# A twelve-stage network on one core: moving a four-bit feed-forward beside the attention that follows it

## The chip, the cores and the metric

The kernel runs on one core of a Trainium2 chip. The metric is the device time of one execution in microseconds. Three runs of the kernel before have a median of 1778.88 us (1777.74 to 1781.62).

## The reference

The network adds twelve sublayers, one after the other, to a residual stream `x` of 2048 tokens by 128 features, in float32. The change lies in two of them, the four-bit feed-forward of the third layer and the linear attention that opens the fourth. Cut to what matters:

```python
def fp4_linear(x, w):
    xq = fp4_quant_dequant(x)      # blocks of 16, scale = max|x| / 6, round to {0, .5, 1, 1.5, 2, 3, 4, 6}
    wq = fp4_quant_dequant(w)
    return jnp.einsum('bsk,nk->bsn', xq, wq)
gate = fp4_linear(x, w_gate)       # 128 -> 352
y = fp4_linear(x, w_up)            # 128 -> 352
h = jax.nn.silu(gate) * y
return fp4_linear(h, w_down)       # 352 -> 128

# the attention behind it
q, k, v = x @ Wq + bq, x @ Wk + bk, x @ Wv + bv          # 128 -> 8 heads of 64
attn = softmax(sum(q_t * k_t) * scale, over heads)       # one weight for each head and token
new_state = decay * state + (1 - decay) * attn * v_t
out = (q * states + sigmoid(q * aug_param)) @ Wo + bo    # then a layer norm
```

Then follow a sublayer that multiplies `sigmoid(r)`, with `r` the normalised stream, by rows that were computed earlier (receptance), and a sparse expert stage with 14 experts.

## The kernel before

All of it is one function, `l2_ffn_and_l3`. The 16 blocks of 128 tokens are taken in four quads of 512 tokens (`NQ = 4`, `QUAD = 4`), and each engine has a program of its own, written out by hand: TensorE makes products and transposes, VectorE (`dve`) rounds, scans and takes statistics, the scalar engine (`act`) copies from PSUM and evaluates sigmoid, silu, exp and gelu, and POOL does the elementwise work left over. An engine works through its program in order. It waits for the others at semaphores: `after(engine, semaphore, n)` and `wait_ge`. So the order of the work is the order of the calls in these four programs.

For a quad `f` the feed-forward goes: `round_x` (eight steps on VectorE: scale, inverse, scaled, step twice, add, subtract), `scale_x_up` (POOL), `turn_x` (four transposes), `take_x` (copy), then for each of the four blocks `gate_up` (line 2698: a gate and an up product, 352 wide), `silu` and `times_gate` (VectorE, line 3052). Gate has bank 5 and up bank 6. Then the rounding of the hidden quad, 1408 wide (`hidden_scales`, `find_steps`, `round_off`, lines 3024 to 3035), `scale_hidden_up` (POOL), `down` (transposes and the 352-row product, line 2718) and `add_down` (line 3061), which adds to `x` and computes the variance for the attention's norm (`spreads`, `variances`, line 239).

The attention of a quad `q`: `turn_attended`, `queries_keys` (lines 2746 and 2747: four chunks of 128 features, two products of 512 columns each), `multiply` (VectorE, line 3109: a key chunk plus bias times the query chunk), scores (line 2755), copy to `s_row`, a small transpose, `subtract_top`, exponential, `shares`, transpose, copy to `probsT`; then for each of the four chunks a value product (2762), a product that spreads the probabilities over the features (2782), and `scan` (VectorE, lines 3128 to 3133: product, recurrence, times query). `add_aug` (POOL) adds the sigmoid; `project` (lines 2727 and 2729) is the output product of one block, four products and a bias row; `take_out`, `stats`, `out_scale`, `apply` and `add_out` (three 128x512 operations on POOL) are its norm. `shifts`, `receptance` and `receive` are the receptance sublayer, and `received_normals` prepares the expert stage.

The feed-forward runs one quad ahead of the attention. At the head of quad `q` the products of the feed-forward for quad `q + 1` and the output product of quad `q - 1` alternate:

```python
for q in range(NQ):
    if q < LAST:
        turn_x(q + 1)
    for j in range(QUAD):
        if q < LAST:
            gate_up(q + 1, j)
        if q > 0:
            project(q - 1, j)
    turn_attended(q)
    queries_keys(q)
    attend(q)
```

`attend(q)` holds `down(q + 1)` between its second and third chunk. After the last quad come `turn_tokens(0)`, `rate(0)` and `first(0, 0)` of the expert stage, the output product of quad 3, and the experts, `second(q, e)` and `first(q, e + 2)` in turn.

## Time and profile before

| what | value |
|---|---|
| median of 3 runs | 1778.88 us |
| the profiled execution | 1774.92 us |
| its span | 1773.1 us |
| TensorE busy (matmuls) | 1524.3 us, 86% |
| TensorE busy with weight loads | 978.7 us, 55% |
| VectorE busy | 1166.1 us, 66% |
| scalar engine busy | 900.9 us, 51% |
| POOL busy | 717.1 us, 40% |

The span is that of the instructions; the execution's own time is 1.8 us longer. Busy shares are averages over twelve sublayers. The function of this case starts at 1272 us of the span; its loop over quads with the lead-in reaches to 1553 us, and the expert stage fills the rest. The hidden quad lies in the tile `w_l_xattn`, the rounded input and the gate values in `ctx`, which are free by then. Matmuls of float32 are shown with two instructions for each product. PE in a view is TensorE, DVE is VectorE, ACT is the scalar engine. A clock of 1.00 is the full 2.4 GHz and 0.50 is 1.2 GHz. In a timeline the bracket at the end says how long the engine had been idle and which instruction released it.

### The profile page before, as it was taken

The numbers are of one execution on the slowest core, as the hardware profiler recorded it, in microseconds if no ns is written. First come the engines' busy times: TensorE is split into PE (matmuls) and PEld (weight loads), VectorE is DVE, ScalarE is ACT, GpSimd is POOL, SyncE is SP. The second block draws the span as 40 slices with busy tenths as digits, with TensorE's granted clock in tenths as the row PEclk, the third lists the DMA queues.
The fourth block names the chain that finished last, engine by engine and source line by source line (L and its number), as shares of the span: only waits on it lengthen the run. The fifth ranks groups of instructions, "written<-read, shape, count | busy, mean of one in ns | idle before, by whom it ended". The sixth has DMA issues, their size and how long they took to land. (4 is left out here: it accounts for less than half of the span.)

```text
span 1773.1 us, 28878 instructions
## 1 busy us (share of the span) xinstructions
PE 1524.3 (86%) x10011; PEld 978.7 (55%) x10011; DVE 1166.1 (66%) x2471; ACT 900.9 (51%) x2612; POOL 717.1 (40%) x674
## 2 busy tenths in 40 slices
PE   4998858789799998979999879999758876789998
PEld 2565535445577765533333358888533443367776
DVE  4887572479687865548989877777636557544443
ACT  2774432267577752247777647776513322444442
POOL 2566341122664433138888953333401235412000
PEclk8999987989999999979999999999857877899999
DMA  6000000000000000020000000000000000000000
GB/s 279 2 2 1 1 1 1 0 1 2 1 2 1 2 1 1 1 85 1 1 1 1 1 1 2 1 2 2 1 1 0 1 1 1 1 1 7 7 1 13
DMA packets 3166, 18.96 MB, mean 11 GB/s; under 512 B 593, under 2 KB 721, under 8 KB 2257
## 3 DMA queue, kind: packets, MB, share of 16 engines
q1 hardware_dynamic: 3024, 17.14, 2.4%
q8 instruction: 81, 1.33, 0.3%
q14 instruction: 61, 0.49, 0.1%
HBM read 16.09 MB, written 1.05 MB: 10 GB/s over the span
## 5 line engine op out<-in xcount | busy, mean ns | idle before, releaser
L827 POOL TENSOR_TENSOR l_xattn_probs<-l_xattn_probs,l_xattn_recip 128x512 f32<-128x512 f32 x128 | 133.0, 1039 | 223.2 <-DVE l_xattn_recip L766 222.8
L999 ACT ACTIVATE l_attn_probs<-ps,l_attn_neg_max 128x128 f32<-128x128 f32 x512 | 144.7, 383 | 74.4 <-DVE l_attn_neg_max L1048 74.1
L2547 POOL TENSOR_TENSOR l_mamba_hc<-l_mamba_h,l_mamba_c 128x512 f32<-128x512 f32 x128 | 159.0, 1269 | 0.0
L2449 DVE TENSOR_TENSOR_SCAN l_mamba_h<-ps,l_mamba_dBx 128x512 f32<-128x512 f32 x128 | 152.7, 1213 | 1.8 <-ACT ps L2346 0.7
L2219 PE MATMUL ps<-l_mamba_hc,w_const 128*128 128x512 f32 x256 | 136.5, 637 | 19.5 <-POOL l_mamba_hc L2547 16.5
L3160 DVE SCALAR_TENSOR_TENSOR xn<-ps,l_gates,xn 128x128 f32<-128x128 f32 x224 | 63.1, 345 | 119.1 <-PE ps L2831 118.2
L761 DVE COPY l_xattn_probsT<-ps 128x512 f32<-128x512 f32 x128 | 88.0, 687 | 71.5 <-PE ps L613 71.5
L2960 ACT ACTIVATE wkv<-ps,w_early 128x512 f32<-128x512 f32 x112 | 70.7, 683 | 115.5 <-PE ps L2820 115.5
L2831 PEld LDWEIGHTS ps<-w_early,wkv 128*128 128x128 f32 x896 | 109.1, 194 | 26.1 <-issue 18.7
L2831 PE MATMUL ps<-w_early,wkv 128*128 128x128 f32 x896 | 111.4, 278 | 6.2 <-ACT wkv L2960 6.2
L712 ACT ACTIVATE l_xattn_probs<-ps,l_xattn_neg_max 128x128 f32<-128x128 f32 x256 | 91.7, 389 | 41.5 <-DVE l_xattn_neg_max L756 41.5
L2820 PE MATMUL ps<-xnT,w_early 128*128 128x512 f32 x224 | 107.8, 605 | 0.0
L712 ACT ACTIVATE l_xattn_probs<-l_xattn_biased,l_xattn_neg_max 128x128 f32<-128x128 f32 x256 | 99.3, 391 | 12.2 <-DVE l_xattn_neg_max L756 12.2
L2346 ACT ACTIVATE ps<-l_mamba_th,l_mamba_a_bias,l_mamba_a_scale 128x508 f32<-128x508 f32 x128 | 97.1, 781 | 14.1 <-DVE l_mamba_h L2449 13.8
L1048 DVE TENSOR_REDUCE l_attn_neg_max<-ps 128x8 f32<-128x1024 f32 x64 | 78.0, 1221 | 32.6 <-PE ps L904 32.6
L245 POOL TENSOR_TENSOR rs<-rs,neg_half 128x4 f32<-128x4 f32 (+2 forms) x28 | 39.4, 1407 | 143.3 <-DVE rs L239 143.3
L2219 PEld LDWEIGHTS ps<-l_mamba_hc,w_const 128*128 128x128 f32 x256 | 44.4, 193 | 86.9 <-POOL l_mamba_hc L2547 70.0
L613 PE MATMUL ps<-w_const,l_xattn_probs 128*128 128x128 f32 x512 | 82.2, 284 | 9.6 <-DVE l_xattn_probsT L761 5.1
L613 PEld LDWEIGHTS ps<-w_const,l_xattn_probs 128*128 128x128 f32 x512 | 57.7, 143 | 51.4 <-issue 39.3
L904 PE MATMUL ps<-l_attn_k_one,l_attn_q 32*128 32x512 f32 x256 | 77.3, 699 | 8.1 <-POOL l_attn_k_one L1079 4.5
L2540 POOL TENSOR_TENSOR l_mamba_dBx<-l_mamba_dtx,l_mamba_b 128x512 f32<-128x512 f32 x48 | 60.9, 1270 | 56.6 <-DVE l_mamba_dtx L2409 36.1
L915 PEld LDWEIGHTS ps<-w_const,l_attn_probs 128*128 128x128 f32 x512 | 58.3, 146 | 42.7 <-issue 28.3
(524 smaller groups left out, 3690.2 us busy)
## 6 DMA issues: line engine op xcount, KB each, us to landing
w_early<-in_l_moe SPq DMA_DIRECT2D x1, 3669.0 KB, 11.5
w_l_xattn<-in_l_xattn SPq DMA_DIRECT2D x1, 2176.0 KB, 22.5
w_early<-in_l_xattn SPq DMA_DIRECT2D x1, 1890.0 KB, 15.1
w_l_attn<-in_l_attn SPq DMA_DIRECT2D x1, 1242.0 KB, 24.5
ctx<-in_ctx SPq DMA_DIRECT2D x1, 1088.0 KB, 10.8
x<-in_x SPq DMA_DIRECT2D x2, 512.0 KB, 4.4
ctxT<-in_ctxT SPq DMA_DIRECT2D x1, 1024.0 KB, 8.9
out_x<-x SPq DMA_DIRECT2D x4, 256.0 KB, 2.2
```

The costliest lines, as they stand in the source:

```text
L613: mm = nc.tensor.transpose(T_of(n)[:, g * P:(g + 1) * P], probs[:, D % 2, n, g, :], G.c["ident"])
L712: ins = nc.scalar.activation(probs[:, D % 2, n, g, :], values, ACT.Exp, bias=neg_max[:, D % 2, n, g:g + 1], accum_out=row_sum[:, D % 2, n, ...
L761: nc.vector.tensor_copy(probsT[:, D % 2, n, :, :], heads4(T_of(n))).then_inc(copied, 1)
L827: nc.gpsimd.tensor_tensor(probs[:, D % 2, n, :, :], probs[:, D % 2, n, :, :], along(recip[:, D % 2, n, :], [P, HALF, P]), ALU.mult).then_i ...
L999: ins = nc.scalar.activation(probs[:, t % 4, g, :], S_of(t)[:, g * P:(g + 1) * P], ACT.Exp, bias=neg_max[:, t % 2, g:g + 1], accum_out=total)
L1048: nc.vector.tensor_reduce(neg_max[:, t % 2, :], by_head(S_of(t), 8), AX.X, ALU.max, negate=True).then_inc(maxed, 1)
L2219: nc.tensor.matmul(G.ps[:, SUM_BANK[half], :], G.c["ident"], hc[:, t % 4, half, :], start=False, stop=n == NS - 1).then_inc((sum0, sum1)[h ...
L2346: nc.scalar.activation(bank4(DA_BANK[half])[:, :, 1:], th[:, q % 2, half, :, 1:], ACT.Exp, scale=a_scale[:, half, n:n + 1], bias=a_bias[:, ...
L2449: nc.vector.tensor_tensor_scan(flat(h[:, t % 2, half, :, :]), G.ps[:, DA_BANK[half], :], flat(dBx[:, t % 2, half, :, :]), 0.0, ALU.mult, A ...
L2547: nc.gpsimd.tensor_tensor(heads4(hc[:, t % 4, half, :]), h[:, t % 2, half, :, :], c_sb[:, t % 3, :, :], ALU.mult).then_inc((hc0_set, hc1_s ...
L2820: mm = nc.tensor.matmul(G.ps[:, 2 * (e % 2) + c, :], we["w1"][:, (e * EC + c) * P:(e * EC + c + 1) * P], G.xnT[:, quad(q), :], start=True, ...
L2831: mm = nc.tensor.matmul(G.ps[:, Y_BANK[e % 2], j * P:(j + 1) * P], hidden[:, e % 2, c, j * P:(j + 1) * P], we["w2"][:, (e * EC + c) * D:(e ...
```

## The change

The arithmetic is the same. What moves:

- Gate and up products get two pairs of banks, (5, 6) and (4, 7). Block 1 may start without block 0 having been taken; block `j > 1` waits for `times_gate` of block `j - 2` and so on (`h_made`). `turn_x` writes bank 4 instead of 7.
- Quad 1's gate products are made before the loop. In the loop `turn_x(q + 2)` and the gate products of quad `q + 2` stand in `attend(q)`, behind the third and fourth spread of the probabilities. The feed-forward's gate products are thus two quads ahead.
- `project(q - 1, ...)` stands between the chunks of `queries_keys(q)`. Its bias is one product, 512 columns wide, ahead of the blocks.
- On VectorE the rounding steps of the hidden quad stand between the four `multiply` steps; `round_x` comes before the first scan, `stats` behind the rounding, `apply` between `subtract_top` and `shares`, and `times_gate` around the last scan.
- On the scalar engine the four sigmoids (`aug`, now with four buffers) come ahead of `s_row`; `receptance(q - 2)` stands behind `s_row`. The receptance of quad 2 comes in the expert stage, right before that of quad 3.
- On POOL `scale_hidden_up` is first in a quad, `receive(q - 2)` stands ahead of `add_out(q - 1)`, and `attended_normals` behind the second `add_aug`.
- `scale_down` and `round_off` are cut into `find_scales`, `scale_down`, `add_steps` and `take_steps_off`, with the same instructions; `x_step` is the head of `h_step`.

```diff
@@ -2689,17 +2690,22 @@
     def turn_x(f):
         pe.wait_ge(x_rounded, f + 1)
-        after(pe, f_added, f)
+        after(pe, p_copied, f - 1)
+        after(pe, h_made, QUAD * f)
         for j in range(QUAD):
             mm = nc.tensor.transpose(G.ps[:, X_BANK, j * P:(j + 1) * P], xq[:, j * P:(j + 1) * P], G.c["ident"])
         mm.then_inc(x_turned, 1)
     def gate_up(f, j):
         pe.wait_ge(x_copied, f + 1)
-        after(pe, h_made, QUAD * f + j)
-        after(pe, h_copied, QUAD * f)
-        nc.tensor.matmul(G.ps[:, G_BANK, 0:I], xqT[:, j * P:(j + 1) * P], wgT, start=True, stop=True)
-        nc.tensor.matmul(G.ps[:, U_BANK, 0:I], xqT[:, j * P:(j + 1) * P], wuT, start=True, stop=True).then_inc(gu_made, 1)
+        if j == 0:
+            after(pe, h_copied, QUAD * f)
+        if j == 1:
+            after(pe, f_added, f)
+        if j > 1:
+            pe.wait_ge(h_made, QUAD * f + j - 1)
+        nc.tensor.matmul(G.ps[:, G_BANK[j % 2], 0:I], xqT[:, j * P:(j + 1) * P], wgT, start=True, stop=True)
+        nc.tensor.matmul(G.ps[:, U_BANK[j % 2], 0:I], xqT[:, j * P:(j + 1) * P], wuT, start=True, stop=True).then_inc(gu_made, 1)
     def turn_hidden(f, j):
         pe.wait_ge(h_rounded, f + 1)
...
@@ -2722,11 +2728,14 @@
     def project(q, j):
         pe.wait_ge(o_set, CH * (q + 1))
-        pe.wait_ge(p_copied, q + 1)
+        if j == 0:
+            pe.wait_ge(p_copied, q + 1)
+            pe.wait_ge(h_made, QUAD * min(q + 3, NQ))
+            nc.tensor.matmul(G.ps[:, O_BANK, :], G.c["ones_row"], w["bo"].unsqueeze(1).broadcast_to([1, QUAD, D]), start=True,
+                             stop=False, skip_group_check=True)
         for c in range(CH):
-            nc.tensor.matmul(G.ps[:, O_BANK, j * P:(j + 1) * P], o[:, c, j * P:(j + 1) * P],
-                             w["wo"][:, c * D:(c + 1) * D], start=c == 0, stop=False)
-        mm = nc.tensor.matmul(G.ps[:, O_BANK, j * P:(j + 1) * P], G.c["ones_row"], w["bo"], start=False, stop=True)
+            mm = nc.tensor.matmul(G.ps[:, O_BANK, j * P:(j + 1) * P], o[:, c, j * P:(j + 1) * P],
+                                  w["wo"][:, c * D:(c + 1) * D], start=False, stop=c == CH - 1, skip_group_check=True)
         if j == QUAD - 1:
             mm.then_inc(out_made, 1)
...
+            if c > 0 and q > 0:
+                project(q - 1, c - 1)
             after(pe, qk_set, CH * q + max(c - 1, 0))
             nc.tensor.matmul(G.ps[:, Q_BANK[c % 2], :], w["wq"][:, c * P:(c + 1) * P], G.xnT[:, quad(q), :], start=True, stop=True)
             nc.tensor.matmul(G.ps[:, K_BANK[c % 2], :], w["wk"][:, c * P:(c + 1) * P], G.xnT[:, quad(q), :], start=True, stop=True)\
               .then_inc(q_made, 1)
+        if q > 0:
+            project(q - 1, QUAD - 1)
     def attend(q):
-        after(pe, out_copied, q)
-        for c in range(CH):
-            pe.wait_ge(qk_set, CH * q + c + 1)
-            mm = nc.tensor.matmul(G.ps[0:H, S_BANK, :], w["heads"][:, c * H:(c + 1) * H], qk[:, c, :], start=c == 0,
-                                  stop=c == CH - 1)
-        mm.then_inc(s_made, 1)
         def v(c):
             after(pe, fed_set, CH * q + max(c - 1, 0))
...
               .then_inc(v_made, 1)
         v(0)
+        after(pe, out_copied, q)
+        pe.wait_ge(h_made, QUAD * min(q + 2, NQ))
+        for c in range(CH):
+            pe.wait_ge(qk_set, CH * q + c + 1)
+            mm = nc.tensor.matmul(G.ps[0:H, S_BANK, :], w["heads"][:, c * H:(c + 1) * H], qk[:, c, :], start=c == 0,
+                                  stop=c == CH - 1)
+        mm.then_inc(s_made, 1)
+        v(1)
         pe.wait_ge(s_copied, q + 1)
         for j in range(QUAD):
             mm = nc.tensor.matmul(G.ps[:, T_BANK, j * H:(j + 1) * H], s_row[:, j * P:(j + 1) * P],
                                   G.c["ident"][0:H, 0:H], start=True, stop=True)
         mm.then_inc(s_turned, 1)
-        v(1)
         pe.wait_ge(p_set, q + 1)
         for j in range(QUAD):
             mm = nc.tensor.transpose(G.ps[0:H, T_BANK, j * P:(j + 1) * P], probs[:, j, :], G.c["ident"])
@@ -2777,10 +2791,17 @@
         for c in range(CH):
             if c == 2 and q < LAST:
                 down(q + 1)
+            if c == 2 and q + 2 < NQ:
+                turn_x(q + 2)
             if c >= 2:
                 v(c)
             nc.tensor.matmul(G.ps[:, P_BANK[c % 2], :], sel_e[:, c * P:(c + 1) * P], probsT[:],
                              start=True, stop=True).then_inc(p_made, 1)
+            if c >= 2 and q + 2 < NQ:
+                gate_up(q + 2, c - 2)
+        if q + 2 < NQ:
+            gate_up(q + 2, 2)
+            gate_up(q + 2, 3)
     def turn_tokens(q):
         pe.wait_ge(m_normed, QUAD * (q + 1))
...
     down(0)
+    turn_x(1)
+    for j in range(QUAD):
+        gate_up(1, j)
     for q in range(NQ):
-        if q < LAST:
-            turn_x(q + 1)
-        for j in range(QUAD):
-            if q < LAST:
-                gate_up(q + 1, j)
-            if q > 0:
-                project(q - 1, j)
         turn_attended(q)
         queries_keys(q)
...
@@ -2921,8 +2938,14 @@
         ins.then_inc(r_set, 1)
     def attend(q):
+        act.wait_ge(q_set, CH * (q + 1))
+        after(act, o_set, CH * q)
+        for c in range(CH):
+            nc.scalar.activation(aug[:, c, :], q_sb[:, c, :], ACT.Sigmoid, scale=w["aug"][:, c:c + 1]).then_inc(aug_set, 1)
         act.wait_ge(s_made, q + 1)
         nc.scalar.copy(s_row[:], G.ps[0:H, S_BANK, :]).then_inc(s_copied, 1)
+        if q > 1:
+            receptance(q - 2)
         act.wait_ge(shifted, q + 1)
         nc.scalar.activation(probs[:], probs[:], ACT.Exp, scale=DH ** -0.5).then_inc(exped, 1)
         act.wait_ge(p_turned, q + 1)
@@ -2930,15 +2953,17 @@
         for c in range(CH):
             if c == 2 and q < LAST:
                 take_hidden(q + 1)
+            if c == 2 and q + 2 < NQ:
+                take_x(q + 2)
             act.wait_ge(v_made, CH * q + c + 1)
             after(act, fed_set, CH * q + max(c - 1, 0))
             nc.scalar.activation(v_sb[:, c % 2, :], G.ps[:, V_BANK[c % 2], :], ACT.Identity,
                                  bias=fresh_bv[:, c:c + 1], scale=fresh[:, c:c + 1]).then_inc(v_set, 1)
-            after(act, o_set, CH * q + max(c - 1, 0))
-            nc.scalar.activation(aug[:, c % 2, :], q_sb[:, c, :], ACT.Sigmoid, scale=w["aug"][:, c:c + 1])\
-              .then_inc(aug_set, 1)
-        if q > 0:
-            receptance(q - 1)
...
             if e == 5:
                 take_gates(q)
             if (q, e) == (0, 5):
+                receptance(LAST - 1)
                 receptance(LAST)
             if e == 10 and q < LAST:
                 take_tokens(q + 1)
...
-    round_off(h_scaled, h_step, h_evened)
+    add_steps(h_scaled, h_step)
+    take_steps_off(h_scaled, h_step, h_evened)
     scale_up(blocks(old[:, 0:QUAD * I]), h_scaled, h_scale[:], h_evened, 0, h_rounded)
     add_down(0)
+    times_gate(1, 0)
     normals(0)
+    for j in range(1, QUAD):
+        times_gate(1, j)
     for q in range(NQ):
         f = q + 1
         if f < NQ:
-            for j in range(QUAD):
-                times_gate(f, j)
+            hidden_scales(f)
+        multiply(q, 0)
+        if f < NQ:
+            hidden_down()
+        multiply(q, 1)
+        if f < NQ:
+            find_steps(h_scaled, h_step)
+        multiply(q, 2)
+        if f < NQ:
+            add_steps(h_scaled, h_step)
+        multiply(q, 3)
+        if f < NQ:
+            take_steps_off(h_scaled, h_step, h_evened)
         if q > 0:
             stats(q - 1)
-        multiply(q)
+        subtract_top(q)
         if q > 0:
             apply(q - 1)
-        if f < NQ:
-            hidden_scales(f)
-        subtract_top(q)
-        if f < NQ:
-            find_steps(h_scaled, h_step)
         shares(q)
-        if f < NQ:
-            round_off(h_scaled, h_step, h_evened)
+        if f + 1 < NQ:
+            round_x(f + 1)
+        scan(q, 0)
+        scan(q, 1)
         if q > 1:
             received_spreads(q - 2)
-        scan(q, 0)
-        scan(q, 1)
-        if f + 1 < NQ:
-            round_x(f + 1)
+        if f < NQ:
+            add_down(f)
+        scan(q, 2)
         if q > 0:
             attended_spreads(q - 1)
-        scan(q, 2)
-        if f < NQ:
-            add_down(f)
+        if f + 1 < NQ:
+            times_gate(f + 1, 0)
         scan(q, 3)
         if f < NQ:
             normals(f)
+        if f + 1 < NQ:
+            for j in range(1, QUAD):
+                times_gate(f + 1, j)
     below_max(0)
     for q in range(NQ):
         best_two(q)
...
@@ -3310,30 +3359,32 @@
     attended_normals(0)
     for q in range(NQ):
         f = q + 1
+        if f < NQ:
+            scale_hidden_up(f)
         if q > 0:
             out_scale(q - 1)
+        if q > 1:
+            receive(q - 2)
+        if q > 0:
             add_out(q - 1)
+        if f + 1 < NQ:
+            scale_x_up(f + 1)
+        add_aug(q, 0)
+        add_aug(q, 1)
         if f < NQ:
-            scale_hidden_up(f)
+            attended_normals(f)
+        add_aug(q, 2)
+        if q > 0:
+            shifts(q - 1)
+        add_aug(q, 3)
         if q > 1:
             received_normals(q - 2)
-        add_aug(q, 0)
-        add_aug(q, 1)
-        if f + 1 < NQ:
-            scale_x_up(f + 1)
-        if q > 0:
-            shifts(q - 1)
-        add_aug(q, 2)
-        add_aug(q, 3)
-        if f < NQ:
-            attended_normals(f)
-        if q > 0:
-            receive(q - 1)
     out_scale(LAST)
     add_out(LAST)
     shifts(LAST)
+    receive(LAST - 1)
+    receive(LAST)
     received_normals(LAST - 1)
-    receive(LAST)
     received_normals(LAST)
```

TensorE before, at the end of quad 0's attention (value product 2762, spread 2782) and the head of quad 1 (`turn_x` 2694, gate and up 2701 and 2702, output product 2727 and 2729):

```order
L2762 MATMUL ps<-xnT,w_l_attn 128x512
L2782 MATMUL ps<-l_probsT,w_const 128x512
L2694 MATMUL ps<-w_const,ctx 128x128 x4
L2701 MATMUL ps<-w_l_mamba,l_xqT 128x352
L2702 MATMUL ps<-w_l_mamba,l_xqT 128x352
L2727 MATMUL ps<-w_l_attn,l_o 128x128 x4
L2729 MATMUL ps<-w_l_attn,ones 128x128
L2701 MATMUL ps<-w_l_mamba,l_xqT 128x352
L2702 MATMUL ps<-w_l_mamba,l_xqT 128x352
L2727 MATMUL ps<-w_l_attn,l_o 128x128 x4
```

The same place now (`turn_x` 2696, value 2767, spread 2798, gate and up 2707 and 2708):

```order
L2696 MATMUL ps<-w_const,ctx 128x128 x4
L2767 MATMUL ps<-xnT,w_l_attn 128x512
L2798 MATMUL ps<-l_probsT,w_const 128x512
L2707 MATMUL ps<-w_l_mamba,l_xqT 128x352
L2708 MATMUL ps<-w_l_mamba,l_xqT 128x352
L2767 MATMUL ps<-xnT,w_l_attn 128x512
L2798 MATMUL ps<-l_probsT,w_const 128x512
L2707 MATMUL ps<-w_l_mamba,l_xqT 128x352
L2708 MATMUL ps<-w_l_mamba,l_xqT 128x352
L2707 MATMUL ps<-w_l_mamba,l_xqT 128x352
L2708 MATMUL ps<-w_l_mamba,l_xqT 128x352
```

The gate and up products lie ahead of the transpose of the attended quad in both, but the output product has gone from between them. It now stands behind that transpose (2747), with its bias (2734) ahead of the first block (2737), between the query and key products (2757, 2758):

```order
L2747 MATMUL ps<-w_const,xn 128x128 x4
L2757 MATMUL ps<-xnT,w_l_attn 128x512
L2758 MATMUL ps<-xnT,w_l_attn 128x512
L2734 MATMUL ps<-w_l_attn,ones 128x512
L2737 MATMUL ps<-w_l_attn,l_o 128x128 x4
L2757 MATMUL ps<-xnT,w_l_attn 128x512
L2758 MATMUL ps<-xnT,w_l_attn 128x512
L2737 MATMUL ps<-w_l_attn,l_o 128x128 x4
L2757 MATMUL ps<-xnT,w_l_attn 128x512
```

VectorE before, at the head of quad 1, from the four key products on (`multiply` 3109, `apply` 3089, scales 3024 to 3027, `subtract_top` 3115):

```order
L3109 SCALAR_TENSOR_TENSOR l_qk<-ps,w_l_attn,l_q 128x512 x4
L3089 TENSOR_SCALAR l_out<-l_out,l_small 128x128 x4
L3024 TENSOR_REDUCE l_h_scale<-w_l_xattn 128x88
L3025 TENSOR_SCALAR l_h_scale<-l_h_scale 128x88
L3026 RECIPROCAL l_h_inverse<-l_h_scale 128x88
L3027 SCALAR_TENSOR_TENSOR w_l_xattn<-w_l_xattn,l_h_inverse 128x1408
L3115 TENSOR_REDUCE l_top<-ps 128x4
```

and now (scales 3048 and 3049, `multiply` 3144, `scale_down` 3054 and 3055, steps 3058 to 3065):

```order
L3048 TENSOR_REDUCE l_h_scale<-w_l_xattn 128x88
L3049 TENSOR_SCALAR l_h_scale<-l_h_scale 128x88
L3144 SCALAR_TENSOR_TENSOR l_qk<-ps,w_l_attn,l_q 128x512
L3054 RECIPROCAL l_h_inverse<-l_h_scale 128x88
L3055 SCALAR_TENSOR_TENSOR w_l_xattn<-w_l_xattn,l_h_inverse 128x1408
L3144 SCALAR_TENSOR_TENSOR l_qk<-ps,w_l_attn,l_q 128x512
L3058 TENSOR_SCALAR w_l_xattn<-w_l_xattn 128x1408
L3059 TENSOR_SCALAR w_l_xattn<-w_l_xattn 128x1408
L3144 SCALAR_TENSOR_TENSOR l_qk<-ps,w_l_attn,l_q 128x512
L3062 TENSOR_TENSOR w_l_xattn<-w_l_xattn 128x1408
L3144 SCALAR_TENSOR_TENSOR l_qk<-ps,w_l_attn,l_q 128x512
L3065 TENSOR_TENSOR w_l_xattn<-w_l_xattn 128x1408
```

The key products are spread over the rounding, and the rounding's last step comes before the maximum of the scores instead of after the shares.

## Rows read from the trace of the kernel before

**Rows 1.** Stages: busy (instructions) of PE, PEld, DVE, ACT, POOL, then clock.

```profile
1319.66:1374.26 54.60, 43.27 (x113) 20.75 (x112) 32.60 (x54) 17.81 (x32) 10.11 (x8) 0.72 0.00 1
1374.26:1432.96 58.70, 42.78 (x153) 23.29 (x151) 40.25 (x83) 20.25 (x38) 18.57 (x16) 0.82 0.00 0
1432.96:1492.64 59.68, 45.18 (x148) 25.01 (x148) 39.19 (x85) 20.08 (x36) 25.70 (x22) 0.79 0.00 1
1492.64:1553.48 60.84, 46.89 (x153) 27.32 (x153) 25.76 (x66) 17.87 (x27) 26.97 (x24) 0.74 0.00 1
```

**Rows 2.** Timeline of VectorE, lead-in: start, duration, line, tiles [idle before].

```profile
1290.00 0.52 DVE L3052 TENSOR_TENSOR w_l_xattn<-ctx,ps 128x352 f32<-128x352 f32 x1 [3.36 <-ACT ctx L2889]
...
1298.33 1.62 DVE L3024 TENSOR_REDUCE l_h_scale<-w_l_xattn 128x88 f32<-128x1408 f32 x1
...
1307.80 1.62 DVE L3040 TENSOR_TENSOR w_l_xattn<-w_l_xattn,l_h_scale 128x1408 f32<-128x1408 f32 x1
```

**Rows 3.** Groups by line of VectorE in round 1, 1374.26 to 1432.96.

```profile
L3109 DVE SCALAR_TENSOR_TENSOR l_qk<-ps,w_l_attn,l_q 128x512 f32<-128x512 f32 x4 | 3.0, 751 | 4.5 <-ACT l_q L2907 4.5
...
L3052 DVE TENSOR_TENSOR w_l_xattn<-ctx,ps 128x352 f32<-128x352 f32 x4 | 2.1, 518 | 8.6 <-ACT ctx L2889 8.6
```

**Rows 4.** Timeline of TensorE in rounds 1 and 2.

```profile
1387.96 0.86 PE L2701 MATMUL ps<-w_l_mamba,l_xqT 128*128 128x352 f32 x2
...
1389.24 1.05 PE L2727 MATMUL ps<-w_l_attn,l_o 128*128 128x128 f32 x8
...
1394.65 1.02 PE L2747 MATMUL ps<-xnT,w_l_attn 128*128 128x512 f32 x2
...
1399.23 3.60 PE L2755 MATMUL ps<-l_qk,w_l_attn 128*8 128x512 f32 x8
...
1444.73 1.54 PE L2701 MATMUL ps<-w_l_mamba,l_xqT 128*128 128x352 f32 x2
...
1447.24 1.92 PE L2727 MATMUL ps<-w_l_attn,l_o 128*128 128x128 f32 x8
```

**Rows 5.** Timeline of VectorE, end of round 1.

```profile
1420.92 0.68 DVE L3024 TENSOR_REDUCE l_x_scale<-xn 128x32 f32<-128x512 f32 x1
...
1425.80 0.87 DVE L3094 BATCH_NORM_STATS2 st<-x 128x6 f32<-128x128 f32 x4
...
1427.76 0.69 DVE L3128 TENSOR_TENSOR l_fed<-l_v,ps 128x512 f32<-128x512 f32 x1
...
1430.35 0.68 DVE L3061 TENSOR_TENSOR x<-x,ps 128x512 f32<-128x512 f32 x1
```

**Rows 6.** Timeline of the scalar engine.

```profile
1412.55 1.28 ACT L2938 ACT_TABLE_LOAD   x1
1413.85 0.72 ACT L2938 ACTIVATE l_aug<-l_q,w_l_attn 128x512 f32<-128x512 f32 x1
...
1430.56 1.65 ACT L2920 ACTIVATE l_r<-x,l_shift,rs 128x128 f32<-128x128 f32 x4 [5.48 <-POOL l_shift L3290]
```

**Rows 7.** Timeline of TensorE, last output product and sixth expert.

```profile
1547.04 1.59 PE L2727 MATMUL ps<-w_l_attn,l_o 128*128 128x128 f32 x8
...
1584.18 3.78 PE L2831 MATMUL ps<-w_early,wkv 128*128 128x128 f32 x16 [6.17 <-ACT wkv L2960]
```

**Rows 8.** Timelines of POOL and VectorE: operations beside each other and alone.

```profile
1356.38 2.59 POOL L3257 TENSOR_TENSOR w_l_xattn<-w_l_xattn,l_h_scale 128x1408 f32<-128x1408 f32 x1 [33.86 <-DVE w_l_xattn L3035]
...
1439.59 1.26 POOL L3294 TENSOR_TENSOR l_r<-l_r,ctxT 128x512 f32<-128x512 f32 x1
...
1357.36 2.69 DVE L3131 TENSOR_TENSOR_SCAN l_state<-l_keep,l_fed 128x512 f32<-128x512 f32 x1
...
1428.48 1.22 DVE L3131 TENSOR_TENSOR_SCAN l_state<-l_keep,l_fed 128x512 f32<-128x512 f32 x1
```

**Rows 9.** TensorE timeline before its gate products, then its clock over 4 us.

```profile
1431.18 1.09 PE L2694 MATMUL ps<-w_const,ctx 128*128 128x128 f32 x4 [6.66 <-DVE x L3061]
...
1444.00:1448.00 4.00, 4.00 (x11) 0.50 0.02 4
```

58 lines of the change are left out of this document (35 added, 23 removed).

## Prediction

> **What bounds the kernel now.** I read the busy time of the engines by stage, then TensorE's and VectorE's order of time through one quad, then the clock. The page's chain names lines but not rounds, so I cut the span myself: a round runs from the end of one quad's variance (line 239, the last step of `spreads` behind `add_down`) to the next quad's. In the rounds of 54.6, 58.7 and 59.7 us no engine is full [rows 1]: VectorE is busy 40.25 of 58.7 us, TensorE 42.8, and a good part of that at half clock. The rounds are bound by a chain that crosses the engines one at a time. [rows 2] shows one link: VectorE sits 3.4 us before a gate product (L3052), because one pair of banks holds gate and up, so the next pair of products waits for it. In round 1 VectorE loses 8.6 us before those four products and 4.5 us before the key products (L3109), waiting for the scalar engine, which waits for TensorE [rows 3]; that is most of its idle 18 us.
>
> TensorE's costs come at two rates [rows 4]. A gate/up pair goes from 1444.73 to 1447.24, 2.5 us, at half clock, and 1.3 us at full (1387.96 to 1389.24). A token block of the output product is 1.05 us at full clock, about twice that at half; its bias row goes on top. A query/key pair takes 1.7 us at full clock (two products of 1.02 that overlap by 0.16), some 3.5 at half. The scores take 3.6 us. The serial piece on VectorE has its marks in [rows 5]: x rounding 1420.92 to 1425.80 (4.9 us), the spreads of another quad 1425.80 to 1427.76 (1.9), a scan step 1427.76 to 1430.35 (2.6), `add_down` with its variance from 1430.35 to the round's end at 1432.96 (2.6). The rounding of a hidden quad, scales included, took 1298.33 to 1307.80, 9.5 [rows 2].
>
> **The change, part by part.** All times from the profiled execution, 1774.92 us.
>
> Lead-in. With two pairs of banks, quad 0's gate products no longer alternate with VectorE. Today the last ends just before the reduction at 1298.33 [rows 2]. Now four pairs run back to back, held only by VectorE, which is free at 1286.1: product 0 ends 1286.6, pair 2 1289.1, pair 3 1291.6 (2.5 us each at half clock), then 0.6 for the sigmoid and 0.5 for the product: 1292.7. **-5.6 us**.
>
> Round 0 (54.6 now). Quad 1's pairs start at 1318.1 behind quad 0's output, before the variance, and end at +8.4 of the round rather than +13.6. Then the attended transpose and copy (1.3), and the first query/key pair at full clock (+11.3; TensorE has been busy without a gap since +0). The rounding steps now stand between key products: VectorE's queue there holds 3.0 of key products and 9.5 of rounding; the last key product is at +20.8, its score at +21.8. Before `s_row` the scalar engine must now load a table and do four sigmoids, 1.28 + 4 x 0.7 (they overlap to 4.1) [rows 6]: it is free at +22.5. So scores leave at +23.1, 1.5 later the maximum is off, then exponential, shares (+25.6), x rounding 4.9, two scans 5.3, sum and variance 2.6: +38.4. I add 1.1 for waits on POOL (below): 39.5. **-15.1 us**.
>
> Round 1 (58.7 now), the steady one. VectorE first does scan 2 (2.6), the spreads of the attended quad (1.9), one gate product (0.5), scan 3 (2.6), its normals (0.7) and gate product 1: +8.9. Only then may TensorE issue pair 3, since pair 3 waits for product 1, and `turn_attended` stands behind it. At half clock: pair 3 to +11.4, transpose 1.1, copy 0.7, query/key pair 3.5: +16.6. Bias and first block 3.7, then, at full clock, three query/key pairs and two blocks (7.3) to +27.6, the last block and first value product 2.0, scores 3.5: +33.1; the sigmoids end at +33.5. Copy, turn and maximum 2.1: +35.6. `apply`, which ran in an idle gap, now stands here with 1.0, shares 0.7: +37.3. x rounding 4.9, scans 5.3, sum and variance 2.6: +50. POOL adds 2: **52**, so **-6.7**. At full clock throughout the same chain is 5 shorter. The rounding of the hidden quad (9.5) and the four key products (3.0) fit into the 20 us in which VectorE waits for TensorE: this is what is hidden. If TensorE were faster there, that cover would end near 15 us and VectorE would be next.
>
> Round 2 (59.7 now). As round 1, less x rounding (4.9), but the first spread probabilities are then 2.2 late, the spreads of the received quad add 1.9, and `receptance` (1.65 [rows 6]), moved from the end of a quad to between `s_row` and the exponential, exceeds its cover by 0.9: again 50, and 52 with POOL. **-7.7**.
>
> Tail, from the last variance to the first second product of the expert stage (60.8 now). The four blocks of quad 2's output product move from ahead of the queries to between them and the score chain gains some 4 us. But the last scans end later against the expert stage's first products, which used to cover them, so quad 3's output product, 54.4 into this stretch now (1547.04 [rows 7]), waits for them: +55 with POOL, then 5.1 at full clock or 9.8 at half. I take 61: **0**, with ends 56 and 66.
>
> Expert stage. `receptance` of quad 2 now stands right before that of quad 3, with one buffer `r`. The second waits for POOL's `receive` of quad 2, which in POOL's queue is behind `shifts` of quad 3: two 128x512 operations of 1.26 us [rows 8] and a link, 2.6. TensorE already sits 6.17 us there [rows 7], so all of it shows: **+2.6**.
>
> The bias as one 512-wide product instead of four costs about the same columns: 0. The DMAs don't move.
>
> The price of POOL. A scan that starts within POOL's 2.59 us operation (1356.38 to 1358.97) takes 2.69, not 1.22, and ends 1.1 after POOL's does; it waits it out [rows 8]. Today `add_out`'s three operations lie beside one reduction and score waits. Now they lie beside shares and x rounding, on the path. Least: 0, if they fall into gaps; most: 3.8 + 0.8, all three and one link in series. I take 2, nearer the middle, since part of x rounding starts before them. The Trainium skill ("SBUF — State Buffer", who interferes with whom) has it as a lock: a VectorE instruction with two SBUF inputs, or in a two-port mode, and a POOL instruction that reads SBUF exclude each other for a whole instruction. The scan row agrees. By that rule nearly every step of the rounding can block, so rounds 1 and 2 would pay 4.6, not 2: 1751.6 for the whole. That is part of a rival below.
>
> Sum: -5.6 - 15.1 - 6.7 - 7.7 + 0 + 2.6 = -32.5, 1742.4 on the profiled execution. The median of the runs is 4.0 above it: **1746.4**.
>
> **The rivals.**
> *The clock stays up.* The gate products lie between the value products, so gaps are shorter than the 6.66 us before 1431.18, after which the clock is at 0.50 (1.2 GHz) until past 1448 [rows 9]. For it: the pairs of round 0 are gapless. Against: TensorE still waits twice, for products 0 and 1. Then rounds 1 and 2 are 47 and the tail 56: -15, 1731.
>
> *POOL's operations serialise at the slow clock.* Rounds of 55 and 56 and a tail of 66: +12, 1758. For it: the scan row. Against: POOL's operations are paced by links and a step may get in first.
>
> *Slower.* TensorE's queue is in order: pair 3 waits for VectorE behind two scans, and the transpose, queries, output blocks and scores behind pair 3. If these gaps keep the clock low through the scores, round 1 pays 3 x 1.8 more for query/key pairs, 3 x 1.0 for blocks and 3.5 for scores: 52 + 12 = 64, above 58.7. With rounds 1 and 2 at +24, round 0 +9, tail +8: 1746 + 41 = 1787. It decides where these losses together pass the 32.5 gained. Against: in [rows 4] scores at 1399.23 run at full clock some 20 us after a low start.
>
> *Not hidden.* If `add_down` comes late, pair 1 also waits for it and three pairs rather than one lie on the path, 2.5 each in rounds 1 and 2: +10, 1756. In the range.
>
> **How the numbers follow.** Forecast 0.5, clock up 0.2, POOL or not hidden 0.25, slower 0.04, the rest gains of under 15. The ends of the range are the first two rivals, 1731 and about 1762 (1758 and 4 for the spread of a tail that is both late and slow); outside lies less than 0.2. A measurement of this kernel tells 0.2%, 3.6 us, from no change. Faster 0.95, same 0.01, slower 0.04.
>
> **What would show it.** L3052 ending near 1292.7 in the lead-in; variances 39, 52 and 52 us apart; the copy of the scores near +34 of rounds 1 and 2; scans and x steps above their plain durations beside POOL; TensorE's gap of 6.17 us at the sixth expert grown to near 9. Wrong would be middle rounds above 57, or a wait ahead of `turn_attended` of over 14 us.

## The result

The changed kernel takes 1749.84 us (median of 4 runs, 1747.32 to 1753.47), the kernel before 1778.31 on the same chip (4 runs, 1777.41 to 1781.62): ratio 0.9838, 95% interval 0.9813 to 0.9864. It is 28.5 us faster and 3.4 above the forecast of 1746.4. The profiled execution took 1747.32 us with a span of 1745.5, against 1774.92 and 1773.1 before.

The span is cut as in [rows 1], with the stretch before round 0 and the expert stage added. In order the rows are lead-in, rounds 0, 1 and 2, tail, expert stage.

```profile
1275.70:1314.41 38.71, 20.06 (x90) 14.43 (x91) 28.55 (x59) 11.00 (x26) 5.66 (x5) 0.74 0.00 0
1314.41:1350.13 35.72, 30.98 (x107) 15.18 (x106) 27.86 (x50) 16.99 (x31) 8.86 (x7) 0.90 0.00 1
1350.13:1403.98 53.85, 45.59 (x152) 24.24 (x151) 40.63 (x72) 20.32 (x35) 16.69 (x13) 0.78 0.00 0
1403.98:1456.47 52.49, 40.38 (x141) 20.98 (x139) 40.82 (x86) 19.18 (x35) 20.98 (x17) 0.80 0.00 0
1456.47:1523.06 66.59, 42.59 (x141) 22.32 (x142) 33.64 (x80) 18.00 (x27) 31.16 (x31) 0.74 0.00 1
1523.06:1745.50 222.44, 208.26 (x1202) 152.44 (x1200) 92.20 (x374) 90.48 (x140) 19.66 (x21) 0.97 0.02 6
```

| stage | before | after | difference | forecast |
|---|---|---|---|---|
| up to the start of `l2_ffn_and_l3` | 1272.11 | 1275.70 | +3.6 | 0 |
| lead-in | 47.55 | 38.71 | -8.8 | -5.6 |
| round 0 | 54.60 | 35.72 | -18.9 | -15.1 |
| round 1 | 58.70 | 53.85 | -4.9 | -6.7 |
| round 2 | 59.68 | 52.49 | -7.2 | -7.7 |
| tail | 60.84 | 66.59 | +5.8 | 0 |
| expert stage | 219.62 | 222.44 | +2.8 | +2.6 |
| span | 1773.1 | 1745.5 | -27.6 | -32.5 |

The first line of the table is not the change's: nothing there was edited, and in the kernels below that start lies anywhere from 1269.97 to 1282.96. The stages that the forecast is about give -31.2 together.

**Lead-in and round 0.** TensorE's timeline, gate and up products of quad 0, then the last of quad 1 and the turn of the attended quad:

```profile
1286.05 1.38 PE L2707 MATMUL ps<-w_l_mamba,l_xqT 128*128 128x352 f32 x2
...
1290.38 0.83 PE L2707 MATMUL ps<-w_l_mamba,l_xqT 128*128 128x352 f32 x2 [1.78 <-DVE w_l_xattn L3085]
...
1292.23 0.75 PE L2708 MATMUL ps<-w_l_mamba,l_xqT 128*128 128x352 f32 x2
...
1317.45 0.76 PE L2708 MATMUL ps<-w_l_mamba,l_xqT 128*128 128x352 f32 x2
1318.05 0.60 PE L2747 MATMUL ps<-w_const,xn 128*128 128x128 f32 x4
```

Quad 0's four pairs come two by two without a gap inside the two, and the second two (1.3 us a pair) and all of quad 1's run at 2.4 GHz. Quad 1's pairs end 3.8 us into round 0, where the forecast had 8.4.

**Round 1.** TensorE around the last gate/up pair, and then the waits in VectorE's groups (compare [rows 3]):

```profile
1358.54 1.51 PE L2707 MATMUL ps<-w_l_mamba,l_xqT 128*128 128x352 f32 x2 [3.63 <-DVE w_l_xattn L3085]
...
1362.75 2.07 PE L2757 MATMUL ps<-xnT,w_l_attn 128*128 128x512 f32 x2 [0.68 <-ACT xnT L2918]
...
1368.46 2.08 PE L2737 MATMUL ps<-w_l_attn,l_o 128*128 128x128 f32 x8
...
1374.82 1.02 PE L2757 MATMUL ps<-xnT,w_l_attn 128*128 128x512 f32 x2
```

```profile
L3144 DVE SCALAR_TENSOR_TENSOR l_qk<-ps,w_l_attn,l_q 128x512 f32<-128x512 f32 x4 | 3.0, 750 | 8.2 <-ACT l_q L2924 8.2
...
L3085 DVE TENSOR_TENSOR w_l_xattn<-ctx,ps 128x352 f32<-128x352 f32 x4 | 2.0, 511 | 2.9 <-ACT ctx L2906 2.9
```

Waits before gate products fell from 8.6 us to 2.9, but those before key products rose from 4.5 to 8.2: VectorE now waits for TensorE at half clock (in e1 below, where the same round runs at full clock, they are 2.3). The scalar engine's copy of the scores (round 1, round 2, tail) stands at +34.7, +31.3 and +32.1 of its stage:

```profile
1384.85 0.58 ACT L2946 COPY l_s_row<-ps 8x512 f32<-8x512 f32 x1
...
1435.23 0.57 ACT L2946 COPY l_s_row<-ps 8x512 f32<-8x512 f32 x1
...
1488.56 0.57 ACT L2946 COPY l_s_row<-ps 8x512 f32<-8x512 f32 x1 [0.15 <-PE ps L2776]
```

**POOL beside VectorE.** VectorE in the lead-in, where POOL is idle, and then the same steps of x rounding, the last step of the shares (L3157) and two scans in round 1, beside `add_out` and other operations of POOL:

```profile
1286.13 0.18 DVE L3049 TENSOR_SCALAR l_x_scale<-l_x_scale 128x32 f32<-128x32 f32 x1
...
1286.74 0.69 DVE L3055 SCALAR_TENSOR_TENSOR l_x_scaled<-xn,l_x_inverse 128x512 f32<-128x512 f32 x1
...
1388.74 1.04 DVE L3157 TENSOR_TENSOR l_probs<-l_probs,l_top 128x32 f32<-128x32 f32 x1
...
1390.42 0.70 DVE L3049 TENSOR_SCALAR l_x_scale<-l_x_scale 128x32 f32<-128x32 f32 x1
...
1391.54 1.44 DVE L3055 SCALAR_TENSOR_TENSOR l_x_scaled<-xn,l_x_inverse 128x512 f32<-128x512 f32 x1
...
1395.99 1.58 DVE L3166 TENSOR_TENSOR_SCAN l_state<-l_keep,l_fed 128x512 f32<-128x512 f32 x1
...
1398.93 1.80 DVE L3166 TENSOR_TENSOR_SCAN l_state<-l_keep,l_fed 128x512 f32<-128x512 f32 x1
```

L3157 takes 0.19 where nothing is beside it (e3 below, round 1, at 1384.38), and a scan 1.22 [rows 8]. So the price is 0.85 + 0.52 + 0.75 + 0.36 + 0.58 = 3.1 us, where I took 2 out of 0 to 4.6. Of it the first three, 2.1 us, lie beside `add_out`, whose price the 2 was; the two scans, 0.9 us, lie beside `scale_x_up` and `add_aug`, which that term left out.

**Tail and expert stage.** TensorE: turn of the last quad, last output product (bias, then 32 products), sixth expert.

```profile
1465.95 1.12 PE L2747 MATMUL ps<-w_const,xn 128*128 128x128 f32 x4 [9.71 <-DVE xn L260]
...
1516.03 2.07 PE L2734 MATMUL ps<-w_l_attn,ones 1*128 1x512 f32 x2 [7.40 <-POOL l_o L3320]
1518.03 5.19 PE L2737 MATMUL ps<-w_l_attn,l_o 128*128 128x128 f32 x32
...
1556.29 3.78 PE L2852 MATMUL ps<-w_early,wkv 128*128 128x128 f32 x16 [8.81 <-ACT wkv L2985]
```

### The profile page after: what moved, and what is told of

Its sections match the earlier page's. It is cut to its first block and busy times, and to the rows that moved or that the text cites. A ratio compares the mean times of both kernels' runs of the same rounds, so it can differ in the third digit from the quotient of the medians.

```text
span 1745.5 us, 28828 instructions
## 1 busy us (share of the span) xinstructions
PE 1506.1 (86%) x9987; PEld 965.2 (55%) x9987; DVE 1171.3 (67%) x2471; ACT 902.2 (52%) x2612; POOL 716.9 (41%) x674
## 3 DMA queue, kind: packets, MB, share of 16 engines
q1 hardware_dynamic: 3024, 17.14, 2.4%
## 5 line engine op out<-in xcount | busy, mean ns | idle before, releaser
L1048 DVE TENSOR_REDUCE l_attn_neg_max<-ps 128x8 f32<-128x1024 f32 x64 | 78.1, 1221 | 32.5 <-PE ps L904 32.5
```

The source lines that it names most:

```text
L1048: nc.vector.tensor_reduce(neg_max[:, t % 2, :], by_head(S_of(t), 8), AX.X, ALU.max, negate=True).then_inc(maxed, 1)
```

## The experiments

Each kernel is the changed kernel with one edit, or with several where that is said. The stages of their profiled executions (the first expert product's place moves in three of them, so tail and expert stage are summed), with the median of all runs, their extent, and the ratio to the kernel before with its interval. e1, e2, e6 and e7 shared one chip, e3, e5 and e8 another, e9 to e11 a third. Each ratio is against the kernel before on the same chip, whose median there was 1776.43, 1770.78 and 1773.85 (1774.76 beside e11), so medians of different chips are not to be compared.

| kernel | lead-in | round 0 | round 1 | round 2 | tail + experts | median us | ratio |
|---|---|---|---|---|---|---|---|
| before | 47.6 | 54.6 | 58.7 | 59.7 | 280.5 | 1778.31 | 1 |
| after | 38.7 | 35.7 | 53.9 | 52.5 | 289.0 | 1749.84 (1747 to 1753) | 0.984 (0.981 to 0.986) |
| e1 receive first | 39.0 | 35.7 | 46.6 | 52.5 | 286.2 | 1743.68 (1741 to 1745) | 0.981 (0.976 to 0.986) |
| e2 one bank pair | 47.5 | 44.2 | 54.1 | 56.3 | 289.6 | 1772.56 (1765 to 1777) | 0.996 (0.994 to 0.999) |
| e6 rounding behind | 38.7 | 36.9 | 55.1 | 60.3 | 289.1 | 1758.66 (1753 to 1765) | 0.991 (0.987 to 0.995) |
| e7 output whole | 39.0 | 35.4 | 53.5 | 59.0 | 287.7 | 1748.49 (1747 to 1760) | 0.986 (0.980 to 0.992) |
| e3 apply behind | 39.0 | 35.7 | 47.2 | 50.8 | 284.7 | 1742.54 (1738 to 1749) | 0.985 (0.979 to 0.992) |
| e5 tail order | 38.7 | 35.7 | 50.5 | 52.5 | 283.5 | 1739.48 (1736 to 1747) | 0.983 (0.977 to 0.990) |
| e8 filled, 24 and 18 | 38.8 | 35.7 | 53.9 | 52.5 | 289.3 | 1742.50 (1741 to 1749) | 0.985 (0.979 to 0.991) |
| e11 filled, 16 and 10 | 38.7 | 35.7 | 53.9 | 52.5 | 282.2 | 1740.11 (1735 to 1749) | 0.983 (0.979 to 0.986) |
| e9 = e1 + e3 + e5 | 39.0 | 35.7 | 47.2 | 50.8 | 277.1 | 1734.01 (1730 to 1738) | 0.978 (0.974 to 0.982) |
| e10 = e9 filled | 38.7 | 35.7 | 54.4 | 50.8 | 274.5 | 1728.14 (1720 to 1734) | 0.974 (0.969 to 0.978) |

Up to round 2, the stages that an edit does not touch repeat within 0.4 us, except round 1, on which see e1; the last column moves by up to 1.1 where nothing in it was edited. So I read the edits from the stages; the intervals of most medians overlap.

### e1: the order of receive and shifts

```
-            shifts(LAST)
             receive(LAST - 1)
+            shifts(LAST)
```

> One step of POOL's queue moves: receive of quad 2 stands ahead of shifts of quad 3 instead of behind it. Theory (two receptances share one buffer, the second waits for the first receive behind shifts): TensorE's idle time at the sixth expert falls from 8.81 us back to 6.2, the expert stage from 222.4 to 219.8, the kernel by 2.6. Rival (the gap has grown for another reason, a late variance or table load): nothing changes, 8.8 us stay.

The expert stage fell from 222.44 to 219.48 us, with the wait at the sixth expert back at its old 6.17. TensorE's timeline of e1, at that place:

```profile
1554.12 3.78 PE L2852 MATMUL ps<-w_early,wkv 128*128 128x128 f32 x16 [6.18 <-ACT wkv L2985]
```

This term of the forecast is shown: 3.0 us, all from POOL's queue. What nobody had touched is round 1, 46.64 us instead of 53.85. TensorE's timeline of e1, and its window over the round:

```profile
1366.09 0.83 PE L2707 MATMUL ps<-w_l_mamba,l_xqT 128*128 128x352 f32 x2 [3.62 <-DVE w_l_xattn L3085]
...
1368.62 1.12 PE L2757 MATMUL ps<-xnT,w_l_attn 128*128 128x512 f32 x2 [0.68 <-ACT xnT L2918]
```

```profile
1357.69:1404.33 46.64, 38.39 (x152) 20.92 (x151) 40.60 (x72) 20.29 (x35) 16.65 (x13) 0.93 0.00 1
```

The same products stand behind the same idle time (3.62 us here, 3.63 in the changed kernel), and run at full clock here and at half there. Everything else is alike: VectorE busy 40.60 and 40.63 us. So 7.2 us of round 1 hang on whether the clock falls in that gap. The round was of the long kind in the changed kernel, e2, e6, e7, e8, e10 and e11 (53.5 to 55.1 us) and of the short in e1, e3 and e9 (46.6 to 47.2). In e5 (50.5) the clock fell in the gap and came back sooner. The edits do not sort these rounds, but their place in the span does: among the eight kernels whose work is the same up to this gap (all but e2, e6 and e7), the round is long where it starts at 1344.42, 1345.81, 1346.93 or 1350.13 (e11, e8, e10, the changed kernel), 50.5 at 1351.54 (e5), and short at 1352.77, 1353.59 and 1357.69 (e9, e3, e1). No run moves that place alone, so this is an order seen in eight profiles and not a shown cause.

### e2: one pair of banks

```
-        G_BANK, U_BANK, ... = (5, 4), (6, 7), ...
+        G_BANK, U_BANK, ... = (5, 5), (6, 6), ...
...
-                if j > 1:
-                    pe.wait_ge(h_made, QUAD * f + j - 1)
+                if j > 0:
+                    pe.wait_ge(h_made, QUAD * f + j)
```

> The changed kernel with one pair of banks for gate and up again; the order of all work stays. Theory (the pair of banks is what the lead-in and round 0 gained by, the loop less so): the lead-in returns from 38.7 to some 45, round 0 from 35.7 to near 45, rounds 1 and 2 grow by 2 to 4 each, since now pairs 1, 2 and 3 wait for gate products; together +20. Rival (placement alone gave the gain): lead-in and round 0 grow by under 5 together.

Lead-in 47.5 us as before, rounds 0 and 2 +8.4 and +3.8, round 1 +0.3: 21 us up to the tail, where 20 was expected, and a ratio of 0.996. Round 1 was of the long kind in both kernels. VectorE's and TensorE's timelines of e2 in the lead-in show the old alternation, and with it the half clock:

```profile
1298.59 0.52 DVE L3085 TENSOR_TENSOR w_l_xattn<-ctx,ps 128x352 f32<-128x352 f32 x1 [3.36 <-ACT ctx L2906]
```

```profile
1299.26 1.51 PE L2707 MATMUL ps<-w_l_mamba,l_xqT 128*128 128x352 f32 x2 [1.20 <-DVE w_l_xattn L3085]
```

The second bank pair carries most of the gain, and part of it is the clock: in the lead-in it is at half for the alternating pairs and at full for the second two of the gapless ones. How the 21 us divide between the alternation and the clock no run separates.

### e6: rounding behind the key products

```
                 multiply(q, 0)
-                if f < NQ:
-                    hidden_down()
...
                 multiply(q, 3)
                 if f < NQ:
+                    hidden_down()
+                    find_steps(h_scaled, h_step)
+                    add_steps(h_scaled, h_step)
                     take_steps_off(h_scaled, h_step, h_evened)
```

> The changed kernel with the four key products first on VectorE and the hidden quad's rounding (7.6 us) behind all four. Theory (the rounding is hidden in the waits for TensorE): the maximum of the scores is reached 3 us late in round 0 (rounding ends 7.6 after the last key product, the scores are due 4.7 after it) and, with the statistics of 3.5 behind it, about 5 late in rounds 1 and 2: +13. Rival (VectorE has slack there anyway, and the spreading of the steps is worth nothing): under +3.

Rounds 0, 1 and 2 cost 1.2, 1.3 and 7.8 us more, 10.3 together, where 13 was expected. That round 1 lost only 1.3 is the clock again: here it rose after the first query/key pair (1.02 us each from 1368.03), where the changed kernel had two slow pairs and a slow output block. TensorE's waits for the probabilities in rounds 1 and 2 of e6 show the rounding on the path; in the changed kernel they are 2.99 and 4.84:

```profile
1391.21 1.02 PE L2788 MATMUL ps<-w_const,l_probs 128*8 128x128 f32 x4 [8.55 <-DVE l_probs L3157]
...
1451.22 1.02 PE L2788 MATMUL ps<-w_const,l_probs 128*8 128x128 f32 x4 [10.57 <-DVE l_probs L3157]
```

### e7: the output product whole

```
-                    if c > 0 and q > 0:
-                        project(q - 1, c - 1)
...
                 turn_attended(q)
+                if q > 0:
+                    for j in range(QUAD):
+                        project(q - 1, j)
                 queries_keys(q)
```

> The changed kernel with the output product's four blocks in one piece behind the attended transpose, ahead of the query and key products. Theory (the blocks fill gaps between key products only in part, because TensorE is the one waited for): the first key product is late by 5 to 8, but the rest of the block follows faster, and the scores come at the same time: within 2 us of the changed kernel. Rival (splitting is worth its place, VectorE's rounding hides behind it): VectorE's rounding is pushed behind the scores, +3 to +5 in each of rounds 1, 2 and the tail, +12.

Round 1 and what follows round 2 stay within 1.4 us of the changed kernel, round 2 is 6.5 longer. TensorE's timeline of e7, round 2:

```profile
1416.01 6.44 PE L2737 MATMUL ps<-w_l_attn,l_o 128*128 128x128 f32 x32
1422.29 1.02 PE L2755 MATMUL ps<-xnT,w_l_attn 128*128 128x512 f32 x2
```

The queries wait for the whole product, mostly at half clock, and in round 2 the changed kernel had full clock there. In round 1, where both were slow, order makes no difference. How much of the 6.5 is order and how much clock stays open; the ratios (0.986 against 0.984, with overlapping intervals) show no gain by the split.

### e3: shares before apply

```
                 subtract_top(q)
+                shares(q)
                 if q > 0:
                     apply(q - 1)
-                shares(q)
```

> VectorE divides the probabilities of a quad by their sum (shares, which ends in the copy that TensorE waits for) before it applies the norm of the quad before, where the changed kernel applies first. Theory: in the tail the four applies stand on the path in front of the shares, and each is stretched beside GpSimd's receive (2.96 us for the four where 1.11 were seen without it), so taking them off gives 2 to 3 us in the tail (66.6 to about 64) and about 1 to 3 us in round 2; round 1, where x is rounded behind them, stays. Sum -3 to -6 us, expert stage unchanged, as the tokens of quads 0 to 2 are needed only later. Rival: nothing in these places was on the path (what follows the shares, turn and spread, is waited for behind the apply anyway), so the stages stay within 0.5 us each; or slower, by the tokens of quad 2 coming later to the steps of the shift behind them.

Round 2 fell by 1.7 us and the tail by 3.2 (66.59 to 63.35), as the theory had it. The mechanism, in the changed kernel's tail: POOL's `receive` and VectorE's `apply`.

```profile
1490.76 1.26 POOL L3343 TENSOR_TENSOR l_r<-l_r,ctxT 128x512 f32<-128x512 f32 x1 [3.26 <-ACT l_r L2937]
```

```profile
1387.30 1.11 DVE L3125 TENSOR_SCALAR l_out<-l_out,l_small 128x128 f32<-128x128 f32 x4
...
1491.00 2.96 DVE L3125 TENSOR_SCALAR l_out<-l_out,l_small 128x128 f32<-128x128 f32 x4
```

With shares first, TensorE's wait for the probabilities in the tail is 2.90 instead of 4.84 (e3's timeline):

```profile
1485.98 0.60 PE L2788 MATMUL ps<-w_const,l_probs 128*8 128x128 f32 x4 [2.90 <-DVE l_probs L3157]
```

That is 1.9 us, and about the 1.7 of round 2. The rest of the tail's difference is clock, both ways: fewer products were slow behind the turn (20.95 us from the turn of the last quad to the small transpose of its scores, not 23.56), and more in the last output product (6.24 us for its 32, not 5.19).

### e5: expert products ahead of the last output product

```
             first(0, 0)
+            second(0, 0)
+            first(0, 1)
             for j in range(QUAD):
                 project(LAST, j)
...
-                    if (q, e) == (0, 0):
-                        take_out(LAST)
+                    if (q, e) == (0, 1):
                         exponentials(0)
+                        take_out(LAST)
```

> The second product of the first expert and the first of the second stand ahead of the output product of the last quad on TensorE, and on ScalarE the first exponentials ahead of taking the output. Theory: TensorE idles 7.40 us before the last output product while it waits for GpSimd's l_o; the moved products (some 1.95 + 1.8 us at full clock) fill half of it, so the expert stage as a whole ends 3 to 4 us earlier, and up to 7 if the idle time had also cost the clock (the output product there took 5.19 us for 32, at half of the clock). Span 1739 to 1742. Rival: the expert stage is bound by ScalarE's gelu chain and the last output product is on its path by the receive (8.8 us wait at the sixth expert), so what TensorE does earlier is waited out later: within 1 us of the changed kernel.

Tail and expert stage together fell from 289.0 to 283.5 us, 5.6. TensorE's timeline of e5 in place of the 7.40 us wait:

```profile
1509.33 2.05 PE L2852 MATMUL ps<-w_early,wkv 128*128 128x128 f32 x16 [2.69 <-ACT wkv L2986]
...
1514.03 1.12 PE L2734 MATMUL ps<-w_l_attn,ones 1*128 1x512 f32 x2 [0.93 <-POOL l_o L3321]
```

The rival, that a later wait takes it back, is out. The clock is not steady here either: the bias takes 1.12 us, at full clock, yet the 32 products behind it take 5.47, where 3.84 is full clock (e11 below).

### e8 and e11: what the clock costs in the tail

Unread products fill TensorE's idle stretches of 9.71 and 7.40 us: in e8 24 and 18 of them, in e11 16 and 10.

```
+                if q + 2 == NQ:
+                    keep_busy(4, 0, I, 24)
+            def keep_busy(bank, lo, hi, n):
+                for _ in range(n):
+                    nc.tensor.matmul(G.ps[:, bank, lo:hi], xqT[:, 0:P], wgT[:, 0:hi - lo], start=True, stop=True)
...
             first(0, 0)
+            keep_busy(4, 0, I, 18)
```

> Adds products whose result nobody reads: 24 products of 352 columns into a free bank behind the spread shares of round 2, where TensorE idles 9.71 us, and 18 before the output product of the last quad, where it idles 7.40. Nothing else changes. Theory: the tail came out 6 us above the forecast because TensorE's idle 9.71 us dropped the clock to half (query and key pairs 2.07 and 1.91 us, where 1.12 and 1.02 at full), so with the fill the pairs of the last quad take 1.02 to 1.12 us, the tail falls from 66.6 to 61 to 63, and the output product of 32 falls from 5.19 to about 3.4. Span 1738 to 1742. Rival: the query and key products of the last quad are waited out by VectorE's rounding or the spread shares anyway, or the clock drops whatever stands before: the tail stays at 66 to 67 and the pairs at 1.9 or more; or the filling products run at half clock themselves (0.6 us each, 14 us) and delay the turn of the last quad by about 4 us.

TensorE's timeline of e8: the fill (L2810 is `keep_busy`), and the first query product behind it.

```profile
1451.77 14.36 PE L2810 MATMUL ps<-w_l_mamba,l_xqT 128*128 128x352 f32 x48
...
1467.25 1.12 PE L2757 MATMUL ps<-xnT,w_l_attn 128*128 128x512 f32 x2 [0.68 <-ACT xnT L2925]
```

The pairs run at full clock, and from the turn to the small transpose of the scores takes 18.8 us instead of 23.6; but each product took 0.6 us at full clock, twice what I had reckoned, so the turn came 4.4 us late and the tail at 67.1. e11 mends that:

> The changed kernel with the unread products cut to the length of the idle stretches: 16 ahead of the last quad's turn (9.6 us, where 9.71 were idle) and 10 before the last output product (6.0 of 7.4), where 24 and 18 held the pairs at 1.02 us but came 4.3 and 3.4 us too late. Theory: from the last quad's turn to its scores takes 18.8 us as with 24, where the changed kernel took 23.6, and the turn is not late, so the tail comes to 62 and the output product of 32 to 3.84 instead of 5.19: span 5 to 6 us below the changed kernel's with the same middle rounds, near 1739 to 1740. Rival: the clock falls in a kernel like this at a place of its own choosing (with 16 and the other orders, the first pair still took 1.91, and without any fill it took 2.07 and only that pair), so the 18.8 come back only in part: tail 64 to 66.

TensorE's timeline of e11, and its tail:

```profile
1450.37 9.63 PE L2810 MATMUL ps<-w_l_mamba,l_xqT 128*128 128x352 f32 x32
1460.22 0.66 PE L2747 MATMUL ps<-w_const,xn 128*128 128x128 f32 x4 [0.22 <-DVE xn L260]
1461.56 1.13 PE L2757 MATMUL ps<-xnT,w_l_attn 128*128 128x512 f32 x2 [0.68 <-ACT xnT L2925]
...
1506.67 3.84 PE L2737 MATMUL ps<-w_l_attn,l_o 128*128 128x128 f32 x32
```

```profile
1450.74:1510.34 59.60, 51.16 (x192) 28.38 (x191) 33.63 (x80) 18.00 (x27) 31.17 (x31) 0.91 0.00 1
```

Rounds 1 and 2 are those of the changed kernel within 0.02 us (53.85, 52.47), and the tail is 59.60 us, 7.0 shorter: 4.7 between turn and scores, 2.3 in the last output product. The theory's 62 had left out the second. So between these two profiles the half clock costs 7.0 us in the tail, with no other work changed. How much of it the fill itself bought is less sure. The tail of e11 starts at 1450.74 and that of the changed kernel at 1456.47; e9 below has no fill, its tail starts at 1450.74 too, and there only the first query/key pair is slow (TensorE's timeline of e9):

```profile
1462.00 2.07 PE L2757 MATMUL ps<-xnT,w_l_attn 128*128 128x512 f32 x2 [0.68 <-ACT xnT L2919]
```

It takes 20.96 us from turn to small transpose, and e3 20.95. So behind the turn the fill is worth 4.7 us against the changed kernel and 2.1 against these. e8's and e11's own profiled executions also show how weakly one profile speaks of the median: theirs are 1743.20 and 1734.65, their medians 1742.50 and 1740.11.

### e9 and e10: a version that beats both

> The three orders that helped alone, together: receive of quad 2 before the last shifts (-3.0 us in the expert stage alone), shares before the apply of the quad before (-1.7 in round 2 and -3.2 in the tail), and the first two expert products ahead of the last output product (-5.6 over tail and expert stage). If they act in different places they add up: round 2 near 51, tail and expert stage together 289.0 - 3.2 - 3.0 - 5.6 = 277, span near 1732 with round 1 at half of the clock (54) and near 1725 where it is at full clock there (47); TensorE's wait at the sixth expert stays near 6.2. Rival: two of them cover the same wait (the earlier tokens of quads 2 and 3 and the earlier first experts both end at the same later wait for a normed quad), so that together they give no more than 8 of the 12 us: tail and expert stage 281 or more.

The three orders add up: tail and expert stage are 277.1 us, where 277 was expected, round 2 is 50.8, and 1734.01 us in the median.

> The same with products whose result nobody reads: 16 of 352 columns in TensorE's idle stretch before the last quad is turned (18 such took 10.8 us and 24 took 14.4, so 16 take 9.5 of the 9.7 that are idle) and 4 (2.4 us) where 2.7 were idle before the second product of the first expert. Theory: the tail's excess over the forecast is the clock that drops in that idle stretch: with 24 such products the query and key pairs ran in 1.02 to 1.12 us but the turn came 4.3 us late; with 16 it is in time and the pairs still run at full clock, so the tail is 4 to 4.5 us shorter than with the three orders alone. Rival: the clock falls in spite of it, or the score is waited for by something else: less than 1 us.

The profiled tail fell by 0.7 us and the expert stage by 1.8; the tail was to fall by 4 to 4.5. The rival stands, and e9 shows why: it takes 20.96 us from turn to small transpose and 3.84 for the last output product, so some 2.1 was all that a full clock could still win there. In e9 only the first query/key pair was slow (2.07 us for its first product), and in e10 it was slow too (1.91), although the idle stretch was filled but for 1.06 us.

e10's median, 1728.14, is the lowest, but its interval overlaps e9's. Its profiled round 1 was of the slow kind (54.4 us) and e9's of the quick (47.2), which hides most of what separates the two spans (1726.6 and 1727.8). Both ratios lie below the changed kernel's 0.984 (0.981 to 0.986): e10 clear of it, while e9's interval (0.974 to 0.982) still touches it.

## Why the prediction was right, and where its steps were not

The time, the sign and the order of the terms held: two middle rounds of 54 and 52 us, a large gain in lead-in and round 0, a loss in the expert stage. That the total is so close is luck in part: of the six stages two gained 7.0 us more than forecast and four 8.3 less, which leaves 1.3, and another 3.6 lie in the unedited part ahead of them. Step by step:

- **Lead-in, -5.6, came -8.8.** "Four pairs run back to back" held, but for the 1.78 us in which TensorE waits for VectorE, which the forecast had named; "2.5 us each at half clock" failed. The clock rose with the gapless pairs (in e2 it did not), so the second two took 1.3 each, and the last gate product ended 18.3 us into the lead-in (1294.04) rather than 20.6. Another 1.0 was won behind the rounding, where transposes and down products up to the variance take 9.2 us, not 10.2.
- **Round 0, -15.1, came -18.9.** The failed term is the end of quad 1's pairs, 8.4 in the forecast and 3.8 measured, again the pairs' size. Of these 4.6, 3.8 reached the end of the round. The order of links behind it was right.
- **Round 1, -6.7, came -4.9.** The scores' copy is at +34.7, where the sum had 33.5: it took the clock as full from +20.3 on, behind the first output block, and it came back near +24, so the second query/key pair was slow too. That is 1.2 us, POOL (3.1 for 2) is 1.1 more, and 0.4 was made up behind. But e1, e3 and e9 show that the round has a second level, 46.6 to 47.2, the 47 of the first rival; between the levels lie 7.2 us, where the forecast had 5. I put the whole of that rival at 0.2; in this round alone it came in 3 of 11 profiles.
- **Round 2, -7.7, came -7.2,** with two errors that cancel. Queries and keys ran at full clock (scores at +31.3, not 34), and what followed was slower, above all `apply` on the path, 2.95 us beside POOL for 1.11 alone; taking it off the path gave 1.7 in e3.
- **Tail, 0, came +5.8.** "The score chain gains some 4 us" is the step that failed. The copy of the scores was at +29.8 of this stretch before, is at +32.1 now, and at +27.4 in e11: at full clock the chain gains 2.4 us, and with the half clock behind TensorE's 9.71 idle us it loses 2.3. So the last output product starts at +59.6, where the forecast had +55 (e11: +54.9), and its bias and first third run at half clock too, 7.0 us in all between my 5.1 and 9.8. By e11 the clock's part of this is 7.0 us; at full clock the tail is 59.6, with the stretched `apply` (1.9 by e3) still in it. I had named the clock as the end of 66 and took 61.
- **Expert stage, +2.6, came +2.8.** POOL's order, shown by e1 (3.0).
- **The bias at 0 and the hidden rounding** hold: e6 shows what the rounding costs when not hidden.

Of the rivals, "POOL serialises" is real at 3.1 us in round 1, between my 2 and its 4.6. The Trainium skill ("SBUF — State Buffer", who interferes with whom) speaks of a lock for a whole instruction; the trace agrees (L3112 in the last section ends 0.02 us after POOL's operation). My reading of it, that nearly every rounding step would block, did not come about: the later steps of x rounding stood where POOL had nothing to do. "Slower" was never near: the wait ahead of the last pair was 3.63 us and the clock returned before the scores.

## What to carry to other kernels

Price each product on a chain at both rates, and ask of each idle stretch of TensorE ahead of it how often the clock falls there; in this kernel that alone moves a round by 7 us with no edit, so one profile of each kernel does not settle a difference of that size. A second buffer can be worth more than the alternation it removes, where it makes products gapless. Before moving an in-order engine's step, read what the other engines' queues hold beside it: three such reorderings here (e9) gave 13.7 us in round 2, tail and expert stage.

## What the runs showed of the hardware that I had not expected

- **The same gap, either clock.** Behind an idle time of 3.62 us the same product took 0.83 us in e1, e3 and e9 and 1.51 in e8, e10 and e11. What decides it was not found; the quick ones are those that stand latest in the span (see e1). I tried no fill there, since no bank is free.
- **A tiny VectorE instruction waits out a POOL operation.** In round 1 of the changed kernel (VectorE, then POOL):

```profile
1383.24 1.87 DVE L3112 TENSOR_TENSOR l_small<-l_st 128x4 f32<-128x4 f32 x1
```

```profile
1382.50 2.59 POOL L3306 TENSOR_TENSOR w_l_xattn<-w_l_xattn,l_h_scale 128x1408 f32<-128x1408 f32 x1 [24.63 <-DVE w_l_xattn L3065]
```

  Four elements a partition take 1.87 us and end at 1385.11, as POOL's operation ends at 1385.09; the next such instruction (L3113) takes 0.15.
- **A product of 352 columns in f32 takes 0.60 us at full clock:** 24 of them stand as 48 instructions in the trace of e8 and took 14.36 us.
